# Transformer kernel, first stage: pipeline of three steps against four, normalisation on DVE against ACT, and added products on PE

## The reference

```
q, k, v = x W_q, ctx W_k, ctx W_v                 (layer-normed x for q)
scores  = q k / sqrt(128);  attn = softmax(scores)
x       = x + tanh(g_xattn[0]) * attn v
logits  = layernorm(x) W_router                   (top 2 of 8 experts, softmax weights)
x       = x + tanh(g_ffn[0]) * sum over experts
```

## Time and profile before

| | us |
|---|---|
| median of 3 runs | 767.61 (767.25 to 768.88) |
| the profiled execution's own time | 765.61 |
| its span | 763.8 |
| PE busy in the span | 653.7 (86%) |
| DVE busy | 566.9 (74%) |
| ACT busy | 427.8 (56%) |
| POOL busy | 94.4 (12%) |
| mean granted clock of TensorE | 0.909 |

### The profile page before, as it was taken

One profiled execution on the slowest core, in us unless ns is written; L12 is line 12 of the kernel. 1 busy time (PEld: TensorE's weight loads), 2 busy tenths in 40 slices (PEclk: granted clock), 3 DMA queues, 4 the chain that ended last, 5 costly groups with the idle time before them and its releaser, 6 DMA issues.

```text
span 763.8 us, 12816 instructions
## 1 busy us (share of the span) xinstructions
PE 653.7 (86%) x4094; PEld 504.1 (66%) x4094; DVE 566.9 (74%) x1275; ACT 427.8 (56%) x665; POOL 94.4 (12%) x125
## 2 busy tenths in 40 slices
PE   5686665799999999994798988988988379999996
PEld 4574443687778778773576766766765258888884
DVE  3767576888889889887577766866865678888885
ACT  3243221577777777772376666665765045555553
POOL 3344230200000000003001011011001100000000
PEclk9657665899999999998599999999999589999998
DMA  5322000000000000003233313413400000000000
GB/s 160 101 81 82 27 8 0 1 1 0 1 0 0 0 0 0 0 1 98 61 101 102 104 41 95 113 35 90 111 2 1 0 1 0 15 14 14 27 14 28
DMA packets 23698, 29.24 MB, mean 38 GB/s; under 512 B 3313, under 2 KB 17522, under 8 KB 23666
## 3 DMA queue, kind: packets, MB, share of 16 engines
q1 hardware_dynamic: 23666, 28.84, 13.3%
HBM read 19.99 MB, written 8.85 MB: 38 GB/s over the span
## 4 chain that ended last, share of the span: by engine, by line
PE 67%; DVE 18%; issue 5%; POOL 5%; ACT 4%; DVEq 1%; DMA 0%; SPq 0%; ACTq 0%; POOLq 0%
PE psum L371 12%; PE psum L373 12%; PE psum L372 12%; PE psum L1160 5%; PE psum L1175 3%; PE psum L1150 2%; DVE xn L300 2%; DVE stats L281 2%; POOL rstd L293 2%; PE psum L1151 2%; PE psum L360 2%; PE psum L1466 2%; PE psum L858 2%; PE psum L319 1%; DVE a_rg L632 1%
## 5 line engine op out<-in xcount | busy, mean ns | idle before, releaser
L1270 ACT ACTIVATE c_pt<-psum 77x512 f32<-77x512 f32 x128 | 74.6, 586 | 57.4 <-PE psum L1160 57.3
L371 PE MATMUL psum<-xh,w_hi 128*128 (+1 forms) x248 | 102.0, 411 | 2.6 <-DVE d_hr L1554 2.6
L372 PE MATMUL psum<-xl,w_hi 128*128 (+1 forms) x248 | 99.1, 400 | 0.0
L373 PE MATMUL psum<-xh,w_lo 128*128 (+1 forms) x248 | 98.9, 399 | 0.0
L813 DVE TENSOR_TENSOR b_hl<-b_hs,b_hh 128x1024 fp32r<-128x1024 f32 x64 | 78.2, 1222 | 18.0 <-ACT b_hh L807 17.9
L916 ACT ACTIVATE b_hr<-psum,b1s 128x512 f32<-128x512 f32 x128 | 81.1, 686 | 16.8 <-PE psum L373 16.8
L958 DVE TENSOR_TENSOR b_hs<-b_hr,psum 128x1024 f32<-128x1024 f32 x64 | 78.8, 1231 | 12.7 <-ACT b_hr L916 11.5
L807 ACT ACTIVATE b_hh<-b_hs 128x1024 fp32r<-128x1024 f32 x64 | 67.9, 1061 | 34.3 <-PE psum L373 34.1
L1160 PE MATMUL psum<-ident,c_pf 128*77 128x128 f32 x512 | 74.7, 283 | 0.0
L1160 PEld LDWEIGHTS psum<-ident,c_pf 128*77 128x77 f32 x512 | 58.3, 149 | 14.3 <-issue 9.6
L1330 DVE TENSOR_REDUCE c_mx<-psum 128x8 f32<-128x616 f32 x64 | 51.0, 796 | 21.6 <-PE psum L1151 21.0
(11 more groups left out here) (206 smaller groups left out, 1328.0 us busy)
## 6 DMA issues: line engine op xcount, KB each, us to landing
w_hi<-c_q_spread SPq DMA_DIRECT2D x24, 256.0 KB
stage<-in_weights SPq DMA_DIRECT2D x8, 576.0 KB, 4.2
c_q_spread<-w_hi SPq DMA_DIRECT2D x8, 512.0 KB, 3.4
ctxg<-in_ctxT SPq DMA_DIRECT2D x16, 156.0 KB, 4.3
c_k_spread<-w_lo SPq DMA_DIRECT2D x8, 312.0 KB, 2.2
x_all<-in_x SPq DMA_DIRECT2D x8, 256.0 KB, 3.0
out_dram<-x_all SPq DMA_DIRECT2D x8, 256.0 KB, 2.3
c_kb<-c_k_spread SPq DMA_DIRECT2D x48, 39.0 KB
```

Of the source, the lines that this page charges most:

```text
L371: pe.matmul(o, wh, h, start=start, stop=False)
L372: pe.matmul(o, wh, l, start=False, stop=False)
L373: return pe.matmul(o, wl, h, start=False, stop=stop)
L1270: a_.activation(pt[:, q % NC4, :], bank[2 + q % 2][0:S2, :], ACT.Copy).then_inc(pt_done, 1)
```

## The change

- `pipeline4` takes the place of `pipeline` in this stage: eleven steps, `step(a, m, t, u)`. The router's product, its copy, transposes and logits are of group `u`, one step later than before.
- The normalisation of ln0 and ln1 is done by ACT: four activations with scale `rstd` and bias `-mean * rstd` (`act_norm`). POOL makes the bias with two more operations of 128x4 (`pool_shift`). ACT's step begins with it.
- POOL does the ln0 inverse root ahead of the ln1 one.
- PE has a new order, below, and up to three times four products of 128x128 by 128x128 (`keep_busy`) into bank 0. Nothing reads what they write.
- The router's transposes go to the bank of its product, so that product waits until DVE has copied the logits of the group before.

```diff
+def pipeline4(eng, step):
+
+    def groups(i, c):
+        return [Group(i, c - k) if c - k >= 0 and (i is not None or c - k < NG) else None for k in range(4)]
+    for c in range(4):
+        step(*groups(None, c))
+    with eng.Fori(0, (NG - 4) // 2) as i:
+        step(*groups(i, 4))
+        step(*groups(i, 5))
+    for c in range(NG, NG + 3):
+        step(*groups(None, c))
...
+            def pool_shift(self, q, g, nm):
+                _, m, _, rs, _ = self.bufs
+                p = g.parity
+                q.tensor_scalar(nm[:, p, :], m[:, p, :, 0], -1.0, None, ALU.mult).then_inc(self.centred, 1)
+                q.wait_ge(self.rstd_ready, g.at(1, 1))
+                q.wait_ge(self.centred, g.at(1, 1))
+                q.tensor_tensor(nm[:, p, :], nm[:, p, :], rs[:, p, :], ALU.mult).then_inc(self.moved, 1)
+
+            def act_norm(self, a, g, nm):
+                _, _, _, rs, xo = self.bufs
+                p = g.parity
+                a.wait_ge(self.moved, g.at(1, 1))
+                for t in range(TG):
+                    ins = a.activation(xo[:, p, t, :].rearrange("p (a c) -> p a c", a=1), x_all[:, g.tile(t), :], ACT.Identity,
+                                       bias=nm[:, p, t:t + 1], scale=rs[:, p, t:t + 1])
+                ins.then_inc(self.xn_ready, 1)
...
-        lg0 = RouterLogits("a_router", ln1, wg0h, wg0l, bank[7], bank[6])
+        lg0 = RouterLogits("a_router", ln1, wg0h, wg0l, bank[7], bank[7])
+        nm0, nm1 = sb("a_nm0", [P, 2, TG]), sb("a_nm1", [P, 2, TG])
...
         def pool_a(q):
-            def step(a, m, t):
+            def step(a, m, t, u):
+                if a:
+                    ln0.pool_rstd(q, a)
+                    ln0.pool_shift(q, a, nm0)
                 if t:
                     ln1.pool_rstd(q, t)
+                    ln1.pool_shift(q, t, nm1)
                 if a:
-                    ln0.pool_rstd(q, a)
                     pool_split(q, a)
-            pipeline(q, step)
+            pipeline4(q, step)
         pool_parts.append(pool_a)
...
+            def keep_busy(n):
+                for _ in range(n):
+                    pe.matmul(bank[0][:, 0:P], w_m0[:], w_wv0[:], start=True, stop=True)
...
+            def step(a, m, t, u):
+                if m:
+                    scores(m)
+                if u:
+                    if u.i is None and u.c == 0:
+                        pe.wait_ge(s_split, 1)
+                    else:
+                        pe.wait_ge(lg0.lg_copied, u.at(1, 0))
+                    lg0.pe_product(pe, u)
+                if a:
+                    ln0.pe_transpose(pe, a)
+                    keys_values(a)
+                if u:
+                    lg0.pe_transpose(pe, u)
+                if a:
+                    pe.wait_ge(ln0.hi_done, a.at(1, 1))
+                if a and t:
+                    keep_busy(4)
+                if t:
+                    ln1.pe_transpose(pe, t)
+                if m:
+                    if a:
+                        keep_busy(4)
+                    probs(m)
+                    if a:
+                        keep_busy(4)
+                    outs(m)
+            pipeline4(pe, step)
...
-            def step(a, m, t):
+                    ln0.act_norm(a_, a, nm0)
+                if u:
+                    lg0.act_copy(a_, u)
+                    if not t:
+                        Route(0, HEAD, rt_tail).act_ratio(a_)
                 if a:
-                    p = a.parity
-                    a_.wait_ge(a_k_ready, a.at(1, 1))
-                    a_.activation(A["k0"][:, p, :], bank[1][:, 0:GK], ACT.Copy).then_inc(a_k_done, 1)
-                    a_.wait_ge(a_v_ready, a.at(1, 1))
-                    a_.activation(A["v0"][:, p, :], bank[2][0:S2, :], ACT.Copy).then_inc(a_v_done, 1)
+                    ln0.act_high(a_, a)
                 if m:
                     p = m.parity
                     a_.wait_ge(a_sub, m.at(1, 1))
                     a_.activation(A["pr"][:, p, :, :], A["sm"][:, p, :, :], ACT.Exp,
                                   bias=zero_col[:, 0:1], scale=float(D) ** -0.5).then_inc(a_exp, 1)
+                if t:
+                    ln1.act_norm(a_, t, nm1)
+                if a:
+                    a_.wait_ge(a_k_ready, a.at(1, 1))
+                    a_.activation(A["k0"][:, a.parity, :], bank[1][:, 0:GK], ACT.Copy).then_inc(a_k_done, 1)
+                    a_.wait_ge(a_v_ready, a.at(1, 1))
+                    a_.activation(A["v0"][:, a.parity, :], bank[2][0:S2, :], ACT.Copy).then_inc(a_v_done, 1)
+                if t:
+                    ln1.act_high(a_, t)
+                if m:
                     a_.wait_ge(a_pt_ready, m.at(1, 1))
-                    a_.activation(A["pt"][:, p, :], bank[4][0:S2, :], ACT.Copy).then_inc(a_pt_done, 1)
+                    a_.activation(A["pt"][:, m.parity, :], bank[4][0:S2, :], ACT.Copy).then_inc(a_pt_done, 1)
                 if a:
                     act_split(a_, a)
-                if t:
-                    ln1.act_high(a_, t)
-                if a:
-                    ln0.act_high(a_, a)
-                if t:
-                    lg0.act_copy(a_, t)
-                    if not m:
-                        Route(0, HEAD, rt_tail).act_ratio(a_)
-            pipeline(a_, step)
+            pipeline4(a_, step)
...
+            def step(a, m, t, u):
+                if a:
+                    wait_apart(v, s_x[a.parity], a.pair(16, 16))
+                    ln0.dve_stats(v, a)
+                if t:
+                    residual(t)
+                    ln1.dve_stats(v, t)
+                if m:
+                    shift(m)
+                if u:
+                    lg0.dve_copy(v, u)
+                if t and not m:
+                    v.wait_ge(s_split, NG)
+                    v.wait_ge(s_small, 16 * len(small))
+                    v.wait_ge(lg0.lg_copied, NG - 1)
+                    route.first(v)
+                if m:
+                    sums(m)
+                if t:
+                    ln1.dve_low(v, t)
+                    if not m:
+                        route.second(v)
+                if u and not t:
+                    route.weights(v)
+            pipeline4(v, step)
```

More of the change, by code:

```diff
@@ new lines, in scores @@
+            def scores(m):
+                p = m.parity
+                pe.wait_ge(ln0.hi_done, m.at(1, 1))
+                pe.wait_ge(a_k_done, m.at(1, 1))
+                if not (m.i is None and m.c == 0):
+                    pe.wait_ge(a_sub, m.at(1, 0))
+                for b in range(TG):
+                    ins = pe.matmul(bank[3][:, b * SK:(b + 1) * SK], A["xt"][:, p, b * P:(b + 1) * P],
+                                    A["k0"][:, p, b * SK:(b + 1) * SK], start=True, stop=True)
+                ins.then_inc(a_s_ready, 1)
@@ new lines, in keys_values @@
+            def keys_values(a):
+                p = a.parity
+                pe.wait_ge(a_ctx[p], a.pair(16, 16))
+                if not (a.i is None and a.c == 0):
+                    pe.wait_ge(a_k_done, a.at(1, 0))
+                    pe.wait_ge(a_v_done, a.at(1, 0))
+                pe.matmul(bank[1][:, 0:GK], w_m0[:], ctxg[:, p, :], start=True, stop=True).then_inc(a_k_ready, 1)
+                for b in range(TG):
+                    ins = pe.matmul(bank[2][0:S2, b * P:(b + 1) * P], ctxg[:, p, b * SK:b * SK + S2],
+                                    w_wv0[:], start=True, stop=True)
+                ins.then_inc(a_v_ready, 1)
@@ new lines, in probs, with outs @@
+            def probs(m):
+                p = m.parity
+                pe.wait_ge(a_exp, m.at(1, 1))
+                if not (m.i is None and m.c == 0):
+                    pe.wait_ge(a_pt_done, m.at(1, 0))
+                for b in range(TG):
+                    ins = pe.transpose(bank[4][0:S2, b * P:(b + 1) * P], A["pr"][:, p, b, :], ident[:])
+                ins.then_inc(a_pt_ready, 1)
+            def outs(m):
+                p = m.parity
+                pe.wait_ge(a_pt_done, m.at(1, 1))
+                pe.wait_ge(a_v_done, m.at(1, 1))
+                if not (m.i is None and m.c == 0):
+                    pe.wait_ge(a_res, m.at(1, 0))
+                for b in range(TG):
+                    ins = pe.matmul(bank[5][:, b * P:(b + 1) * P], A["pt"][:, p, b * P:(b + 1) * P],
+                                    A["v0"][:, p, b * P:(b + 1) * P], start=True, stop=True)
+                ins.then_inc(a_o_ready, 1)
@@ new lines, in residual @@
+            def residual(t):
+                p = t.parity
+                v.wait_ge(a_o_ready, t.at(1, 1))
+                for b in range(TG):
+                    ins = v.scalar_tensor_tensor(
+                        out=x_all[:, t.tile(b), :], in0=bank[5][:, b * P:(b + 1) * P].rearrange("p (a c) -> p a c", a=1),
+                        scalar=A["rg"][:, p, b:b + 1], in1=x_all[:, t.tile(b), :], op0=ALU.mult, op1=ALU.add)
+                ins.then_inc(a_res, 1)
+                wait_apart(v, a_res, t.at(1, 1))
```

109 lines of the change are left out of this document (19 added, 90 removed).

## The result

| | before | change |
|---|---|---|
| median of 4 runs, us | 767.43 (765.17 to 768.88) | 781.73 (780.17 to 781.93) |
| the profiled execution's own time | 765.61 | 781.76 |
| its span | 763.8 | 780.0 |
| stage, until stage two's weights reach PE | 136.2 | 153.1 |
| the rest of the span | 627.6 | 626.9 |

The change is slower: 1.0177 times the time before, 95% interval 1.0155 to 1.0199, or 14.3 us in the medians. The forecast was 794 within 778 to 810. The sign, the place and the mechanism came out as forecast; the size was 14 where 26 was said.

The account below looks back on a forecast made before the run. The bound was a ring from split to split, 17.2 us a step: last split at 133.5, plus 10.4 and 16.1, plus pauses, ends the stage at 162.4, 26 us later than 136.2. Forecast 794 us, range 778 to 810.

Parts of the forecast that it names:

- The ring: From one POOL split to the next, through ln0 root, shift, ACT normalisation, PE, a_pt and w_hi: 17.2 us a step.
- The bounds of shift and normalisation: Shift on POOL 0.4 to 0.9 us, normalisation on ACT 1.2 to 2.1; over seven steps 5 us either way.
- the rival at 779: PE at full clock all through, kept there by the fillers: 15.1 us a step, 779 us; chance 0.15.
- the signs that were named: Among them: splits 16 to 18 us apart in mid-stage, clock near 0.75, a_rg at 0.23 us, stage about 162 us.
- DVE's hold: DVE's a_rg multiply, held while POOL splits before the change, was to fall to 0.23 us.
- Links off PE: Ring terms on POOL and ACT, among them spare operation, variance and root 1.61 us, shift 0.6, normalisation 1.7.
- PE's groups: ln0 transposes, keys and values, router transposes: 5.0 us; then fillers, ln1 transposes, fillers, probability transposes: 3.4 us.
- The mixed clock: Half clock for PE's first group, full for its second: 17.2 us a step; chance 0.65.
- The allowance of 0.3 us a step: Estimate for pauses between instructions, some six further hand-overs of about 0.05; moved the stage's end from 160.0 to 162.4.
- The rest of the sum: First split at 17.3 us, second 14.1 later, third 16.1; last split to last residual 10.4, then weights 16.1.
- Half clock throughout: PE cooled by the wait at each step's head and never recovering: 19.8 us a step, 812 us; chance 0.11.
- "Faster": POOL's ring doesn't bind; the data's own ring at full clock sets 11.5 us a step, 754 us; chance 0.06.

Follow-up runs that it names:

- kernel 2: The change with w_hi made at the start of ACT's step instead of its end, fillers kept; 757.2 us, ratio 0.9858.
- kernel 3: The change with POOL's split moved a step later, behind the next group's ln0 root and ahead of the older group's ln1 root, fillers kept; 754.1 us, ratio 0.9818.
- Kernel 1: The change without its fillers (the added keep_busy products); 771.7 us, ratio 1.0039.
- kernel 4: The change without fillers, but with twelve of the same products between the router's product and the ln0 transposes; 768.2 us, ratio 1.0000.
- kernel 5: The change with the split behind the next group's ln0 root on POOL and without fillers; 753.5 us, ratio 0.9814.
- kernel 6: As kernel 5, with twelve added products ahead of the ln0 transposes; 759.4 us, ratio 0.9887.
- kernel 8: The kernel before the change, with only w_hi moved to the start of ACT's step; 771.1 us, ratio 1.0043.
- kernel 12: As kernel 5, with both normalisations on DVE; 759.2 us, ratio 0.9907.

## Why the prediction was right in kind and too large

- **The ring** held in every link, and kernels 2 and 3 show it: opening either of its two links takes out more than the whole loss.
- **The number** lies in the range by its width. The bounds of shift and normalisation gave 5 us either way, 789 to 799; 781.7 is inside only because the range was drawn down to the rival at 779, whose full clock throughout didn't come. Of the signs that were named, the splits lie 15.0 to 16.6 us apart in mid-stage, not 16 to 18, the stage has 153.1 us, not 162, and a set of fillers takes 0.89 us from start to start at the full clock, outside the 1.0 to 1.9 within which that step was to hold.
- **DVE's hold** was rightly left out of the sum: a_rg fell from 1992 to 229 ns in the median, and the step grew.
- **Links off PE** were right: root 1.60 (96.96 to 98.56; forecast 1.61), shift and its hand-over to ACT 0.83 (0.6, and part of the 0.5 for hand-overs), normalisation with its hand-over 1.70 (1.7).
- **The step that failed: PE's groups.** For the second, four fillers, transposes, four fillers, transposes, the prediction added durations, 1.06 + 0.66 + 1.06 + 0.66 = 3.4 at the full clock. But a duration runs to the end of the last product, and the next group starts before that: 104.86, 105.75, 106.19, 107.08, 107.52, start to start 0.89 + 0.44 + 0.89 + 0.44 = 2.66. The first group, 5.0 at the half clock, is overrated likewise. In another step, where the half clock stood until 90.4, PE's timeline gives 88.97 - 84.46 = 4.5 from start to start:
```profile
84.46 1.11 PE L350 MATMUL psum<-ident,xn 128*128 128x128 f32 x4 [5.16 <-ACT xn L322]
85.37 1.25 PE L556 MATMUL psum<-ctxg,w_m 128*128 128x312 f32 x2
86.41 1.91 PE L558 MATMUL psum<-w_wv,ctxg 128*77 128x128 f32 x8
88.11 1.06 PE L391 MATMUL psum<-ident,lt_s 128*128 128x128 f32 x4
88.97 1.75 PE L584 MATMUL psum<-w_wv,w_m 128*128 128x128 f32 x8
90.55 0.60 PE L350 MATMUL psum<-ident,xn 128*128 128x128 f32 x4
```
  With the 0.16 us that the last transposes run on, the two groups are 4.5 + 2.8 = 7.3 us at the forecast clocks, where the prediction had 5.0 + 3.4 = 8.4. (Its 1.11 for transposes at the half clock stands in the earlier trace rows as 1.13, which changes nothing.)
  The Trainium skill (page TensorE: Matmul & The Clock Gate, section "Wait — 56ns, not 53.3ns?") gives 55.6 ns from start to start for 128 columns at the full clock and 106.7 at the cold one. The trace agrees with twice that for each record: 0.89 / 8 = 111 ns, and (88.11 - 86.41) / 8 = 213.
- **The mixed clock** was right on average, and its edge wandered. In the step from 94.36 the full clock came back inside the first group, which then took 104.86 - 101.09 = 3.8. The table of stretches:
```profile
101.10:104.10 3.00, 3.00 (x12) 2.54 (x13) 0.00 (x0) 2.28 (x6) 0.21 (x2) 0.50 0.00 0
104.10:109.50 5.40, 5.40 (x51) 5.40 (x50) 2.84 (x15) 3.77 (x7) 0.00 (x0) 1.00 0.00 0
```
  In the step from 77.76 the half clock reached into the fillers instead: 88.97 to 90.55 is 1.6 us for four fillers, which take 0.89 at the full clock. So steps are 15.0 to 16.6 us long. Over the last five, PE's piece from the ln0 transposes to a_pt is 7.33 us on average (6.77, 7.66, 8.06, 6.63, 7.54), which is the sum from start to start at the forecast clocks; that the early and the late edges cancel is luck. Those five steps were 15.8 on average where 17.2 was forecast, 6.9 us of the error, and PE's groups are 8.4 - 7.33 a step or 5.4 in all of it.
- **The allowance of 0.3 us a step** for pauses, 2.4 in all, had no row behind it. The hand-overs were in the links already.
- **The rest of the sum**: first split 16.84 (17.3), second 14.3 later (14.1), third 15.4 (16.1). From the last split (125.66) to the last residual (136.93) 11.3 (10.4), from there to the weights 16.2 (16.1). Together: 7.8 too much up to the last split, 0.9 too little behind it, 2.4 of allowance, 9.3 of the 162.4 - 153.1. A further 2 us of the miss in the medians is the profiled execution of before, which lay 1.8 below its median, while that of the change lay on it; and 0.7 is the rest of the span, 626.9 against 627.6.
- **The rivals.** Full clock throughout (779) came nearest in its number but not in its mechanism: the stage had 0.78, not 1.00. Half clock throughout fell. "Faster" gave 754 for the case that the split is early enough; it isn't in the change, but with the split moved (kernels 2 and 3) the step of 10.8 to 12.5 and the times of 757 and 754 lie near what this rival worked out (11.5, 754). Near in number only: its ring went through residual, transposes and output products, and the chain of waits of kernel 3 goes through POOL, ACT's copies and the ln0 statistics.

Kernel 1 is still 3.7 us slower than before and kernel 4 even with it, though their steps are shorter (14.0 and 13.8 against 14.2). The residuals of kernel 1 say where that lies: the first comes at 29.87, 8.9 later than before, the six steps behind it take 83.9 against 89.5, and the end is 1.7 longer, in all the 4.9 of the stage. In kernel 5, which is kernel 1 with the split moved, the first residual comes at 24.58, so 5.3 of the 8.9 are the split's place as well. What stays open is the other 3.6, up to the 21.02 of before: the order on PE, the shift and the dearer normalisation weren't tried apart there.

## What to carry to other kernels

When work moves between engines, look at which instruction stands last in one engine's step and which stands first behind its consumer on the next: a slow, unhurried operation (here a 2.6 us split whose result only a later stage reads) between them closes a ring. Then work taken off an engine outside the ring (28.3 us of DVE here) is worth nothing, and only shorter links or the opening of the ring count. Moving one instruction past another was worth 24 to 28 us here, while fillers for the clock cost 10 in the closed ring and gave nothing in the open one. Fillers in an engine's idle place aren't free either: at 3.7 to 3.8 us a step they were long enough to lie in the ring that set it (kernels 4 and 6). The filling of the pipeline counts too: more than half of the change's loss came before the first residual. Add PE's groups from start to start, not by their durations.

## What was not expected of the hardware

- The granted clock follows PE's work late. In the change it was 0.97 over 94.4 to 101.1, with PE busy for 1.52 of 6.7 us, and 0.50 over 84.4 to 90.4, with PE busy for 5.94 of 6.0: it falls after the idle piece and comes back after the busy one. So it is the piece behind the idle one that pays, and the mean clock says little of the time: 0.84 at 781.7 us, 0.83 at 753.5.
- Twelve products in PE's idle piece (kernel 4) did not raise the mean clock (0.74, and 0.76 without them). With them output products, scores and router product are at 0.52 (82 to 88 us), and without them the same piece of kernel 1 (84 to 88) is at 1.00: they moved the full clock from one piece of the step to another.
- Of DVE's operations beside POOL's split, the normalisation and the a_rg multiply (scalars from columns, float32 in SBUF) are held (a_rg in the kernel before, median 1992 ns for 229; the normalisation in kernels 8 and 12), while statistics, maximum and the subtraction from PSUM are not (kernel 12). By the Trainium skill (page SBUF — State Buffer, section "SBUF: two separate sides") only some kinds of DVE operation take the shared pair; the rows agree, and name which in this kernel.
